# yq as float16 multiples of 2^-24, two operations in each of POOL's passes, and a new order of loads, PE, ACT and DVE up to the first scales of h

## The reference

```python
U     = (cond_512 @ W_dec + b_dec).reshape(B, 257, 30)      # B = 2
param = einsum('bik,kj->bij', U, V)                          # weight 256 x 256 and a bias row, per batch
y     = x @ param[:, :-1, :] + param[:, -1, :]               # x: 2 x 1024 x 256
h     = gelu(bitlinear(y, w1))                               # w1: 1024 x 256
out   = x + bitlinear(h, w2)                                 # w2: 256 x 1024
# bitlinear(a, w): s = 127 / max|a| of each row (at least 1e-5); aq = clip(round(a s), -128, 127) / s
#                  m = mean|w| of the matrix; wq = clip(round(w / m), -1, 1) m;  aq @ wq.T
```

## Time and profile before

| | us |
|---|---|
| median of 3 executions | 68.99 |
| lowest, highest | 68.6, 71.72 |
| the profiled execution | 68.6 |
| its span (first to last instruction) | 66.8 |
| busy in the span: PE, DVE, ACT, POOL | 57.9, 45.1, 35.8, 28.5 |

### The profile page before, as it was taken

How to read it: one execution, slowest core, us unless ns; L and a number is a source line. 1 busy time by engine, 2 the same in 40 slices (tenths; PEclk the granted TensorE clock), 3 DMA queues, 4 the chain that set the end, 5 groups by cost and what they waited for, 6 DMA issues and landing times.

```text
span 66.8 us, 1289 instructions
## 1 busy us (share of the span) xinstructions
PE 57.9 (87%) x449; PEld 30.0 (45%) x449; DVE 45.1 (67%) x92; ACT 35.8 (54%) x52; POOL 28.5 (43%) x47
## 2 busy tenths in 40 slices
PE   2999999998896799989977959999999999969920
PEld 0325332122332363433513533755849467959800
DVE  2000708565328784899999698599897989996530
ACT  3506006600067297999987644766959393852000
POOL 6400001000000108997939795376493929960000
PEclk9999999999999999999999999999999999999999
DMA  0899999999999999700099959979699969824062
GB/s 0 225 363 417 398 426 418 414 391 386 416 412 427 432 412 427 294 25 0 0 189 59 218 118 194 174 141 182 125 264 181 157 208 309 320 96 157 0 235 79
DMA packets 18342, 16.18 MB, mean 242 GB/s; under 512 B 14752, under 2 KB 15136, under 8 KB 17952
## 3 DMA queue, kind: packets, MB, share of 16 engines
q1 hardware_dynamic: 18192, 15.86, 79.6%
q10 hardware_dynamic: 144, 0.24, 1.5%
HBM read 10.47 MB, written 2.10 MB: 188 GB/s over the span
## 4 chain that ended last, share of the span: by engine, by line
PE 38%; DMA 20%; DVE 15%; SPq 9%; ACT 8%; issue 4%; POOL 2%; DVEq 0%
DMA w_dec_all<-in_w_dec_dram 16%; PE ps_h L463 14%; PE ps_o L483 8%; PE ps_z L483 7%; SPq L249 5%; ACT w_dec_all L607 4%; DMA yq_t<-yq_h 4%; DVE pair_max L713 3%; DVE h_max L731 3%; PE ps_y L435 3%; DVE o_sb L755 3%; SPq L266 2%; PE ps_z L423 2%; POOL hq_h L370 2%; ACT y_q L596 2%
## 5 line engine op out<-in xcount | busy, mean ns | idle before, releaser
L370 POOL TENSOR_SCALAR hq_h<-w_dec_all,pair_rcp 128x1024 f16<-128x1024 f32 x14 | 15.7, 1118 | 7.9 <-DVE pair_rcp L727 7.9
L463 PE MATMUL ps_h<-w_t,yq_t 128*128 128x512 bf16 x64 | 16.0, 380 | 1.2 <-DMA yq_t<-yq_h 0.7
L713 DVE TENSOR_REDUCE pair_max<-w_dec_all 128x2 f32<-128x2048 f32 x7 | 15.9, 2276 | 0.0
L607 ACT ACTIVATE w_dec_all<-ps_h,pair_c 128x1024 f32<-128x1024 f32 x10 | 10.9, 1112 | 6.4 <-PE ps_h L463 6.4
L398 PE MATMUL ps_h<-warm_h 128*128 128x512 bf16 x39 | 13.2, 459 | 1.3 <-POOL warm_h L308 1.3
L463 PEld LDWEIGHTS ps_h<-w_t,yq_t 128*128 128x128 bf16 x64 | 5.5, 98 | 8.6 <-issue 1.3
L483 PE MATMUL ps_o<-w_t,hq_t 128*128 128x256 f16 x64 | 8.3, 273 | 0.6 <-DVE o_sb L755 0.5
L483 PE MATMUL ps_z<-w_t,hq_t 128*128 128x256 f16 x64 | 8.3, 272 | 0.0
L579 ACT ACTIVATE w_abs<-w_sb 128x1024 f32<-128x1024 f32 (+1 forms) x3 | 2.7, 914 | 9.1 <-DMA w_sb<-in_w_tr_dram 9.0
L398 PEld LDWEIGHTS ps_h<-warm_h 128*128 128x128 bf16 x39 | 3.8, 119 | 7.8 <-issue 5.9
L483 PEld LDWEIGHTS ps_o<-w_t,hq_t 128*128 128x128 f16 x64 | 6.0, 98 | 2.6 <-DVE o_sb L755 0.7
(11 more groups left out here) (83 smaller groups left out, 68.8 us busy)
## 6 DMA issues: line engine op xcount, KB each, us to landing
w_sb<-in_w_tr_dram SPq DMA_DIRECT2D x4, 512.0 KB, 8.7
x_sb<-in_x_dram SPq DMA_DIRECT2D x2, 1024.0 KB, 19.0
out_dram<-o_sb SPq DMA_DIRECT2D x7, 256.0 KB, 2.9
w_dec_all<-in_w_dec_dram SPq DMA_DIRECT2D x3, 512.0 KB, 7.5
w_dec_all<-in_w_dec_dram SPq DMA_DIRECT2D x3, 448.0 KB, 8.2
x_t<-in_x_tr_dram SPq DMA_DIRECT2D x1, 1024.0 KB, 16.7
w_dec_all<-in_w_dec_dram SPq DMA_DIRECT2D x1, 576.0 KB, 10.3
x_t<-in_x_tr_dram SPq DMA_DIRECT2D x2, 256.0 KB, 10.9
```

The lines of the kernel that those rows point to most:

```text
L370: pool.tensor_scalar(hq_h[n % NB][:, :], h_tile(n), scale, UNIT, ALU.mult, ALU.mult).then_inc(hq_ready, 1)
L463: last = nc.tensor.matmul(ps_h[k][:, half, :], yq_t[:, p, n % 2, c, :], w1_t[:, c, half * HALF:(half + 1) * HALF], start=(c == 0), stop=(c ...
L607: nc.scalar.activation(h_tile(n), ps_h[n % 2][:, :, :].rearrange("p a n -> p (a n)"), ACT.Gelu, scale=c1_of(n)).then_inc(gelu_done, 1)
L713: nc.vector.tensor_reduce(pair_max[:, p, 2:4], h_pair[p % NH], AXX, ALU.max, apply_absolute_value=True).then_inc(pair_max_ready, 1)
```

## The change

- **Number format.** `quantise_y` writes y as float16 whole multiples of 2^-24, as h is written already: `MAGIC` and `OFFSET` go, the scales of y and h are made with 2^-24 in them, w1's whole numbers become float16. PE transposes float16, `copy_yqt` is a plain copy of 16-bit words, and SP's DMA transposes read `y_q` itself. `narrow_y` (three passes on POOL) and `factor` (two small ones) are gone; from pair 6 on `quantise_y` waits until the DMA transpose that read its buffer has landed.
- **w2.** ACT no longer rounds the first half; POOL's `round_w2` does both halves, and it has two operations (multiply, then minimum with 1) in place of one. `clip_w2` takes the maximum with -1 and multiplies by 1. The magnitudes of w2 are summed on ACT alone, half by half.
- **Order of loads.** The last part of w_dec goes ahead of x_t's first two parts, and x_t's third part (tiles 4 to 7) goes between the halves of w2.
- **Order of PE.** `product_z(1)` comes right behind the first two pairs of y and ahead of `transpose_yq(0)`; four idle matmuls of eight are left there; `transpose_yq(1)` goes behind `product_1(0)` and uses the bank of part 0; `product_y(2)` goes ahead of w2's `total`; `transpose_yq(3)` and `product_y(3)` go between `product_1(2)` and `product_1(3)`.
- **Order of ACT.** `quantise_y(0)`, then the magnitudes of w2's second half (a whole one), `quantise_y(1)`, `gelu(0)`, `quantise_y(2)`, `gelu(1)`, and then as before from `gelu(2)`.
- **Order of DVE.** `add_u_last(1)` comes ahead of pair 1's maxima, pair 2's maxima and scales ahead of w2's scales and `copy_yqt(2)`; the maxima of h's first pair are two instructions, one for each tile.

```diff
@@ SP
-            for n in range(LOADS - 1):
+            for n in range(LOADS):
                 load_wdec(n)
             load_xt(0, 2, s_xt[0])
-            load_wdec(LOADS - 1)
             load_xt(2, 4, s_xt[1])
-            for n in range(2):
-                part = slice(n * HC // 2, (n + 1) * HC // 2)
-                sp.dma_start(w2_sb[:, part, :], w2_tr[:, part, :]).then_inc(s_w2[n], 16)
+            load_w2(0)
             load_xt(4, 8, s_xt[2])
+            load_w2(1)
             load_xt(8, NT, s_xt[3])
...
             def transpose_yq(p):
-                sp.wait_ge(yqh_ready, p - 3)
+                sp.wait_ge(yq_ready, 2 * p + 2)
@@ POOL
-                pool.tensor_scalar(part_of(w2_r, n), part_of(w2_sb, n), s_rcp[:, 1:2], None, ALU.mult).then_inc(s_w2r[n], 1)
+                pool.tensor_scalar(part_of(w2_r, n), part_of(w2_sb, n), s_rcp[:, 1:2], 1.0, ALU.mult, ALU.min).then_inc(s_w2r[n], 1)
...
-                pool.tensor_scalar(part_of(w2_t, n), part_of(w2_r, n), 1.0, -1.0, ALU.min, ALU.max).then_inc(s_w2q[n], 1)
+                pool.tensor_scalar(part_of(w2_t, n), part_of(w2_r, n), -1.0, 1.0, ALU.max, ALU.mult).then_inc(s_w2q[n], 1)
...
-                pool.tensor_scalar(hq_h[n % NB][:, :], h_tile(n), scale, UNIT, ALU.mult, ALU.mult).then_inc(hq_ready, 1)
-
-            factor(0, s_s1)
+                pool.tensor_scalar(hq_h[n % NB][:, :], h_tile(n), scale, 1.0, ALU.mult, ALU.mult).then_inc(hq_ready, 1)
+
             for p in range(AHEAD - 1):
                 scale_y(p)
+            round_w2(0)
+            scale_y(AHEAD - 1)
             round_w2(1)
-            factor(1, s_s2)
-            scale_y(AHEAD - 1)
             for n in range(2):
                 clip_w2(n)
             for p in range(PAIRS):
                 quantise_h(2 * p)
                 scale_pair(p)
-                if 1 <= p < LATE_Y - AHEAD:
-                    narrow_y(p + AHEAD)
                 quantise_h(2 * p + 1)
@@ PE
             product_z(0, (0,))
-            keep_warm(2)
+            keep_warm(1)
             pe.wait_ge(s_usb, len(TURNS))
             product_z(0, (1,))
             keep_warm(1)
             product_y(0)
             product_y(1)
-            keep_warm(4)
-            pe.wait_ge(s_identh, 1)
+            pe.wait_ge(s_xt[2], 16)
+            product_z(1)
+            keep_warm(2)
+            pe.wait_ge(s_identf, 1)
             transpose_yq(0)
-            transpose_yq(1)
-            keep_warm(1)
...
             product_1(0)
-            pe.wait_ge(yqt_copied, 2)
-            pe.wait_ge(s_xt[2], 16)
-            product_z(1)
-            pe.wait_ge(s_w2sum, 3)
+            transpose_yq(1)
+            product_y(2)
+            pe.wait_ge(s_w2sum, 2)
             total(1, w2_sum[:, :])
             transpose_yq(2)
             product_1(1)
-            pe.wait_ge(s_s2, 1)
-            product_y(2)
             product_1(2)
+            transpose_yq(3)
+            product_y(3)
             product_1(3)
             pe.wait_ge(s_xt[3], 16)
+            pe.wait_ge(s_s2, 1)
             product_z(2)
-            transpose_yq(3)
-            product_y(3)
             product_1(4)
@@ ACT
             def quantise_y(p):
                 if p >= 6:
-                    act.wait_ge(yqh_ready, p - 5)
+                    act.wait_ge(yqt_landed[p % 2], yqt_count(p - 2))
...
                     nc.scalar.activation(y_q[p % 2][:, i, :], y_of[p][:, i, 0:D], ACT.Copy,
-                                         bias=MAGIC, scale=scale).then_inc(yq_ready, 1)
+                                         scale=scale).then_inc(yq_ready, 1)
...
+            quantise_y(0)
             act.wait_ge(s_w2sum, 1)
             act.wait_ge(s_w2[1], 16)
-            magnitudes(w2_sb[:, HC // 2:3 * HC // 4, :].rearrange("p t c -> p (t c)"), w2_sum[:, 1:2], s_w2sum)
-            quantise_y(0)
+            magnitudes(w2_sb[:, HC // 2:, :].rearrange("p t c -> p (t c)"), w2_sum[:, 1:2], s_w2sum)
             quantise_y(1)
             gelu(0)
+            quantise_y(2)
             gelu(1)
-            act.wait_ge(s_s2, 2)
-            round_w(w2_r[:, 0:HC // 2, :].rearrange("p t c -> p (t c)"), w2_sb[:, 0:HC // 2, :].rearrange("p t c -> p (t c)"),
-                    s_rcp[:, 1:2], s_w2r[0])
-            quantise_y(2)
             for p in range(AHEAD, NP):
@@ DVE
             copy_yqt(0)
+            add_u_last(1)
             y_maximum(1)
             y_scales(1)
             copy_yqt(1)
-            dve.wait_ge(s_w2[1], 16)
-            magnitudes(w2_sb[:, 3 * HC // 4:, :].rearrange("p t c -> p (t c)"), w2_sum[:, 2:3], s_w2sum)
-            add_u_last(1)
+            y_maximum(2)
+            y_scales(2)
             scales(1, s_s2)
             copy_yqt(2)
-            y_maximum(2)
-            y_scales(2)
+            pair_h_maximum(0, 0, 1)
+            pair_h_maximum(0, 1, 2)
             for p in range(PAIRS):
-                pair_h_maximum(p)
+                if p > 0:
+                    pair_h_maximum(p)
```

More of the change, by code:

```diff
@@ L13 @@
 P = 128
-OFFSET = 16384.0
-MAGIC = 1.5 * 2 ** 23 + OFFSET
 UNIT = 2.0 ** -24
@@ L94, in adaln_ffn @@
         w2_r = sb("w2_r", [P, HC, D], I16)
-        w1_t = sb("w1_t", [P, DC, H], BF16)
+        w1_t = sb("w1_t", [P, DC, H], FP16)
         w2_t = sb("w2_t", [P, HC, D], FP16)
@@ L106, in adaln_ffn @@
         z_t = [sb(f"z_t{k}", [P, P]) for k in range(NQD)]
-        y_q = [sb(f"y_q{k}", [P, 2, D]) for k in range(2)]
-        yq_h = [sb(f"yq_h{k}", [P, 2, D], BF16) for k in range(2)]
-        yq_t = sb("yq_t", [P, NP, 2, DC, P], BF16)
+        y_q = [sb(f"y_q{k}", [P, 2, D], FP16) for k in range(2)]
+        yq_t = sb("yq_t", [P, NP, 2, DC, P], FP16)
         y_inv = sb("y_inv", [P, AHEAD, 2])
@@ L136, in adaln_ffn, with blocks @@
         ps_z = pb("ps_z", [P, 512])
[L138 to L144, removed]
+        def blocks(bank, n):
+            return bank[:, 0:n * P // 2].bitcast(FP16).rearrange("p (c q) -> p c q", c=n)
+        yq_flat = [y_q[k][:, :, :].rearrange("p t c -> p (t c)") for k in range(2)]
         ps_u = [ps_y[:, 0, :], ps_y[:, 1, :], ps_h[1][:, 0, :], ps_h[1][:, 1, :], ps_o]
@@ L160, in adaln_ffn @@
         late_bank = {LATE: ps_y, LATE + 1: ps_h[0], LATE + 2: ps_y, LATE + 3: ps_h[1]}
-        ps_hqt = {n: [blocks(late_bank[n][:, half, :], HC // 2, FP16) for half in range(2)] for n in late_bank}
+        ps_hqt = {n: [blocks(late_bank[n][:, half, :], HC // 2) for half in range(2)] for n in late_bank}
         o_of = [(ps_o, ps_z)[n % 2][:, 0:D] for n in range(NT)]
@@ L190, in adaln_ffn @@
         s_s2 = sem("w2_scale_ready")
-        s_s12 = [sem(f"w{k + 1}_factor_ready") for k in range(2)]
         s_w1r = [sem(f"w1_rounded{a}") for a in range(DC)]
@@ L252, in load_xt, with load_w2 @@
                 sp.dma_start(x_t[:, n0:n1, :, :], x_tr[:, n0:n1, :, :]).then_inc(done, 16)
+            def load_w2(n):
+                part = slice(n * HC // 2, (n + 1) * HC // 2)
+                sp.dma_start(w2_sb[:, part, :], w2_tr[:, part, :]).then_inc(s_w2[n], 16)
             def load_x(b, t0, t1, done):
@@ L315, in _ @@
             pool.wait_ge(s_ident, 1)
-            pool.tensor_copy(ident_h[:, :], ident[:, :]).then_inc(s_identh, 1)
             pool.tensor_copy(ident_f[:, :], ident[:, :]).then_inc(s_identf, 1)
[L319 to L322, removed]
             def scale_y(p):
@@ L334, in scale_pair @@
                 if p == 0:
-                    pool.wait_ge(s_s12[1], 1)
+                    pool.wait_ge(s_s2, 1)
                 pool.tensor_tensor(pair_c[:, p, cols], pair_inv[:, p, cols], s12[:, cols], ALU.mult).then_inc(pair_c_ready, 1)
[L338 to L344, removed]
             def part_of(w, n):
@@ L440, in transpose_yq @@
                 pe.wait_ge(yq_ready, 2 * p + i1)
-                if n > 2:
+                if n > 0:
                     pe.wait_ge(yqt_copied, n)
                 for c in range(DC * i0, DC * i1):
-                    last = nc.tensor.transpose(ps_yqt[n][:, c - DC * i0, :], yq_low[p % 2][:, c * P:(c + 1) * P], ident_h[:, :])
+                    last = nc.tensor.transpose(ps_yqt[n][:, c - DC * i0, :], yq_flat[p % 2][:, c * P:(c + 1) * P], ident_f[:, :])
                 last.then_inc(yqt_done, 1)
@@ L612, in copy_yqt @@
                 p = YQT_PARTS[n][0]
-                nc.scalar.activation(yq_t[:, p, :, :, :].rearrange("p t c q -> p (t c) q"), ps_yqt[n].bitcast(I16), ACT.Copy,
-                                     bias=-OFFSET).then_inc(yqt_copied, 1)
+                nc.scalar.activation(yq_t[:, p, :, :, :].rearrange("p t c q -> p (t c) q").bitcast(I16),
+                                     ps_yqt[n].bitcast(I16), ACT.Copy).then_inc(yqt_copied, 1)
             act.dma_start(small_sb[:, :], small).then_inc(s_small, 16)
@@ L667, in scales @@
                 dve.wait_ge(s_wall, k + 1)
-                nc.vector.tensor_scalar(s_w[:, k:k + 1], w_all[:, k:k + 1], 1.0 / (H * D), EPS,
```

(3 more changed lines are left out.)

41 lines of the change are left out of this document (17 added, 24 removed).

## The result

The changed kernel takes **78.61 us** at the median of four runs (78.28 to 82.95). Before, run beside it, takes 69.59 (68.6 to 71.72). The ratio is 1.141 [1.131, 1.151]. I had forecast 67.6 in 66.8 to 68.9, so the time missed the range by 9.7 us, on the side that I gave 0.11. The profiled run of after took 78.64, with a span of 76.6. Some executions of any of these kernels are disturbed and run a few per cent longer: the ratios leave them out, and as the profiled ones of e1 (73.69), e2 (70.55), e3 (72.81) and b3 (69.95) were of this kind, only starts, durations and, for e2, stretches ahead of the fall of its clock are read from them.

What follows compares the result with a forecast made beforehand. PE's own work bounds the last stage, whose start hangs on a chain from gelu(3) through h's scales, POOL and SP's transposes; that chain comes 1.1 earlier: 68.6 less 1.1 is 67.5, predicted as a 67.6 median, range 66.8 to 68.9.

Steps and rivals of the forecast that it cites:

- The price of POOL's passes: POOL's two-operation w2 roundings: t between 1.04 and 2.85 us each, taken as 1.12 from quantise_h.
- The clips, taken as unchanged: POOL's two clips of w2: priced at 2.1 us together, 1040 ns each, as in the kernel before.
- 27.9 + 2t: When POOL is ready for quantise_h(0), t being one w2 rounding; with t = 1.12 quantise_h(0) starts at 30.1.
- I keep its clock as it is, full: PE with four idle matmuls less: some short gaps, but the clock stays full, so no cost.
- slow rounding: Rival on POOL: roundings stay at 2.85 us, quantise_h(0) starts at 33.6, product_1(8) moves +1.9, total 70.5; chance 0.10.
- a rounding between: Rival on POOL: t between 1.35 and 1.9, quantise_h(0) at 31.1, only 0.6 gained, total 68.0; chance 0.05.
- ACT's path, PE's and DVE's: Paths to h's scales: gelu(3) at 28.9 for 30.01, maxima of pair 1 at 30.05 for 31.18, 1.1 earlier.
- The tie: Start of gelu(3): ACT's path gives 28.89, the path by PE and DVE 28.9 to 29.15; 28.9 taken.
- x_t late: Rival at the loads: x_t's third part lands at 21.4, not 20.2, PE path 0.8 later, total 68.3; chance 0.12.
- Narrow_y, the y transposes and the waits of quantise_y: POOL, SP and ACT: removing narrow_y, y's transposes waiting for ACT and quantise_y's new waits all costed at nothing.
- From gelu(3) to product_1(8) nothing in the chain gets shorter: Chain from ACT's gelu(3) to PE's product_1(8): same length as before, if POOL and SP keep up.
- lost downstream: Rival: SP's transpose queue or the last stage takes back the early gain, total 68.6; chance 0.06.

Runs made afterwards that it cites:

- e1: The changed kernel with w2's clip as before (minimum 1, then maximum -1), roundings still multiply then minimum; 72.79 us, ratio 1.052.
- e2: e1 with both w2 roundings on POOL as two multiplications (by the reciprocal, then by 1); 69.20 us, ratio 1.000 to before.
- e3: e1 with the w2 roundings on POOL as one multiplication, as in the kernel before; 72.18 us, ratio 1.042 to before.
- b3: The kernel before with both w2 roundings on POOL (multiply twice) and ACT's rounding gone, the rest in old order; 69.41 us, ratio 1.005.
- p1: The kernel before with ten extra 128x512 POOL passes in idle time; b and c are one multiplication, to int16 and float16; 70.19 us, single execution.
- e4: e2 with 32 small (32x32) matmuls around transpose_yq(0) in place of two idle ones; 68.60 us, ratio 0.992 to before.
- e5: e2 with six small (32x32) matmuls added behind transpose_yq(0); 68.66 us, ratio 0.993 to before.
- b2: The kernel before with only POOL's pairs changed: its rounding (mult, min), its clips (max, mult); 74.58 us, ratio 1.082.

## Why the prediction was wrong

**The price of POOL's passes**, the step that failed. It said "The nearest row by form is quantise_h, two operations on float32 to 16 bits, 1118 ns" and took that, with the 2852 ns of the one-operation rounding as the upper end. Measured: 3710 ns. (mult, mult) and (mult, min) are not one form on POOL; what these rows shared was the number of operations, and by that the price doesn't go. And a dear row of another pair was no upper bound. The guess on the int16 output was wrong as well (b and c of p1). The two roundings cost 2 x 3.71 in place of 2 x 1.12, so +5.2.

**The clips, taken as unchanged**: "2.1 for the two clips (1040 ns each)". The diff changes their pair from (min, max) to (max, mult), and I priced the old one. Measured 7.24 for the two, +5.1. This was no row too far away but an edit passed over. No rival had it.

**The working behind these two terms held.** "POOL is ready for quantise_h(0) at 27.9 + 2t", with t = 3.71 and 5.14 more for the clips, gives 40.46; measured 40.66. SP's queue adds 4.0, so hq 2's turn is at 44.5 in place of 35.71: 8.8 later, and 68.6 + 8.8 is 77.4. After's profiled run took 78.64. The 1.2 left is the size of what the clock cost, 0.94 and some 0.3; of the rest, 0.24 more lies outside the span (78.64 - 76.6, before 1.8), and yq's pair 4 was issued 8.6 later, not 8.8. Of the clock I wrote only for the four idle matmuls ("I keep its clock as it is, full"); in no rival did I ask what a gap in PE of several microseconds does to it. The *slow rounding* rival, 70.5 for t = 2.85, is e3, at 72.18. Its quantise_h(0) came at 33.78 (forecast 33.6); in its profiled run PE then had a gap of 2.53 and a clock of 0.5 up to some 44.5, and a fetch stalled the first transposes (3.92 of DMA share at 36.5, then 2 GB/s): 2.9 us over before, where I gave it 1.9. Beside the rival *a rounding between* stood the Trainium skill (GPSIMD Engine Reference, 3.1 Elementwise), with an estimate of 1.54 us for a pass. No pass of 1024 elements in any run here lies near it: they take 1.04 to 1.12, 2.85, or 3.63 to 3.71.

**ACT's path, PE's and DVE's** were right. From the start of w2's first magnitudes to the maxima of pair 1 it was 12.20 (31.18 - 18.98) and is 11.22: 0.98 earlier, where I had 1.1. The tie was real: gelu(3) waited 0.22 for PE. x_t came at 20.3 and w2 at 22.7, so *x_t late* didn't occur. b3 shows that the missing rounding alone brings gelu(3) no earlier; the new order with the rounding left on ACT was not run. Narrow_y, the y transposes and the waits of quantise_y show no cost: PE is busy all of 55 to 65.

**"From gelu(3) to product_1(8) nothing in the chain gets shorter"**: in e2's trace it got longer, by the fetch. I had seen that such a fetch can delay a load (in *x_t late*), but not that it can fall among the transposes of pair 2. That is how *lost downstream* came true for e2, which was level with before. In e4 and e5, with the fetch elsewhere, some 0.5 of the 1.1 forecast arrives in the time; in e5's trace product_1(8) is 0.78 earlier.

Part of the rest can be read from the traces. The time outside the span is 2.0 us in e4, e5 and after and 1.8 in before, so 0.2 is lost there; why is open. In e5 a small operation of DVE, 0.17 in before, took 0.80, until POOL's clips ended:

```profile
28.23 2.05 POOL L333 TENSOR_SCALAR w_t<-w_r 128x1024 f16<-128x1024 int16 x2
...
29.50 0.80 DVE L697 TENSOR_SCALAR pair_inv<-pair_max 128x4 f32<-128x4 f32 x1
...
30.66 2.28 DVE L685 TENSOR_REDUCE pair_max<-w_dec_all 128x2 f32<-128x2048 f32 x1
```

So the maxima of pair 1 start at 30.66, in after at 30.24, though both kernels had w2's scale at the same time (POOL's first pass over w2 at 25.88 and 25.91). In e4 that pass came at 26.55: the loads land up to 0.7 us apart from run to run.

## What to carry to other kernels

Price an elementwise pass by the operations in it and their order, not by how many there are or by its types; where the trace has no row of the very pair, measure it first, since a cheap form and a dear one differ by more than any reordering gives. Read a diff for changed operations as closely as for moved ones. When DMA transposes are on the path, look in the trace where instruction fetches fall among them, and don't take one trace's place for the kernel's.

## What was unexpected in the hardware

- POOL's pass with two scalars, 128x512: 0.61 to 0.69 us for (mult, mult), (mult, add) and (min, max); 1.56 for one multiplication; 1.93 to 2.08 for (max, mult), (mult, min) and (max, min). For 1024 elements 1.04 to 1.12, 2.85 and 3.63 to 3.71. A multiplication by 1.0 more makes a pass 2.5 times as fast (2844 to 1117 ns, e3 to e2).
- A fetch of some 20 KB of instructions left DMA transposes in flight at 2 to 77 GB/s for 1.0 to 1.5 us (some 200 beside it), and their landings 0.8 to 1.8 us late. In after, where none was in flight at 32.25, the twelve of h landed in 3.1 to 3.7. Kernels with the same PE list had the fetch up to 4.5 us apart (32.25 and 36.75).
- PE's clock, once at half in a gap, stayed there for six microseconds of dense matmuls (45 to 51 in after).
- A small DVE operation (`pair_inv`, 128x4, 0.17 us in before) took longer beside some passes of POOL, cheap or dear: 0.45 and 0.34 us in after, 0.80 in e5, 1.10 in e1, and mostly it ended as the POOL pass did. In b2, beside dear clips, it took 0.17. What decides it is open.
